# Two-layer graph and attention model on one core: last linear pair by pair, ScalarE's stores behind its copies, gate rows padded to 128

## What is computed

```python
# layer 0: capacity routing
probs = softmax(x @ router_gate);  topw, topi = top_k(probs, 2)
gates = zeros((T, E)).at[arange(T)[:, None], topi].set(topw / (topw.sum(-1, keepdims=True) + 1e-9))
top_g, tok_idx = top_k(gates.T, cap)          # the cap best tokens of each expert
...
# layer 1: the last linear of the graph network, then routing
out = h @ W_self1 + mean @ W_neigh1 + b1      # mean @ W_neigh1 is the last linear, "wn1"
x = x + out + attention(...)
scores = layernorm(x) @ gate_w.T;  top_k(scores, 2); softmax over the two
```

## Time and profile before

| | before |
|---|---|
| median of three runs | 3286.52 us (3283.59 to 3288.06) |
| the profiled execution, its time | 3286.96 us |
| its span, first to last instruction | 3285.1 us |
| mean granted TensorE clock | 0.949 of full |
| TensorE busy | 3052.6 us, 93% of the span |
| VectorE busy | 2019.8 us, 61% |
| ScalarE busy | 1263.2 us, 38% |
| GpSimd busy | 450.1 us, 14% |

### The profile page before, as it was taken

How to read it: one execution, slowest core, us unless ns; L and a number is a source line. 1 busy time by engine, 2 the same in 40 slices (tenths; PEclk the granted TensorE clock), 3 DMA queues, 4 the chain that set the end, 5 groups by cost and what they waited for, 6 DMA issues and landing times.

```text
span 3285.1 us, 53213 instructions
## 1 busy us (share of the span) xinstructions
PE 3052.6 (93%) x22308; PEld 2820.9 (86%) x22308; DVE 2019.8 (61%) x3533; ACT 1263.2 (38%) x2163; POOL 450.1 (14%) x327
## 2 busy tenths in 40 slices
PE   6999999999998899999599999999998999979997
PEld 6998897389987698988499998999998899978887
DVE  6986477977885645444466555766255653645665
ACT  4453055444421034433244334544134421424554
POOL 1033443443000111201000000000000000002222
PEclk9999999999998599999799999999999999968999
DMA  7322112132053266745621000462321333147997
GB/s 251 119 57 43 1 19 54 1 67 67 1 134 114 56 159 175 195 135 155 169 68 40 27 28 28 125 156 79 77 82 62 97 79 104 57 143 229 262 269 208
DMA packets 261920, 344.44 MB, mean 105 GB/s; under 512 B 40706, under 2 KB 223016, under 8 KB 259988
## 3 DMA queue, kind: packets, MB, share of 16 engines
q1 hardware_dynamic: 163351, 191.08, 19.4%
q0 software_dynamic: 43312, 77.14, 11.9%
q10 hardware_dynamic: 54989, 72.35, 7.3%
HBM read 264.10 MB, written 76.40 MB: 104 GB/s over the span
## 4 chain that ended last, share of the span: by engine, by line
PE 86%; DVE 7%; ACT 2%; issue 2%; DMA 1%; ACTq 1%; POOL 0%; DVEq 0%; SPq 0%; POOLq 0%
PE PV L475 18%; PE PV L476 17%; PE PV L477 17%; PE PV L579 6%; PE PS L475 3%; PE PS L476 3%; PE PS L477 3%; PE PV L849 3%; PE PA L503 1%; DVE b L1980 1%; PE PV L755 1%; PE PA L616 1%; DVE b_split L1682 1%; PE PV L795 1%; PE PA L770 1%
## 5 line engine op out<-in xcount | busy, mean ns | idle before, releaser
L475 PE MATMUL PV<-WH,b_split 128*125 128x256 f32 (+2 forms) x3708 | 1086.1, 293 | 94.2 <-DVE b_split L1682 73.9
L476 PE MATMUL PV<-WH,b_split 128*125 128x256 f32 (+2 forms) x3708 | 1073.5, 290 | 2.5 <-issue 2.5
L477 PE MATMUL PV<-WH,b_split 128*125 128x256 f32 (+2 forms) x3708 | 1072.2, 289 | 0.0
L1682 DVE TENSOR_TENSOR b_split<-b,b_split 128x500 fp32r<-128x500 f32 x1040 | 687.7, 677 | 424.5 <-ACT b_split L1288 411.3
L1288 ACT CAST b_split<-b 128x500 fp32r<-128x500 f32 x1040 | 626.0, 613 | 786.0 <-PE PV L477 732.2
L475 PEld LDWEIGHTS PV<-WH,b_split 128*125 128x125 f32 (+2 forms) x3708 | 698.3, 188 | 118.8 <-issue 72.3
L476 PEld LDWEIGHTS PV<-WH,b_split 128*125 128x125 f32 (+2 forms) x3708 | 701.6, 189 | 12.7 <-issue 2.7
L477 PEld LDWEIGHTS PV<-WH,b_split 128*125 128x125 f32 (+2 forms) x3708 | 698.6, 188 | 11.4
L1671 DVE TENSOR_TENSOR WH<-WS,WH 128x1024 fp32r<-128x1024 f32 x292 | 344.3, 1221 | 128.0 <-ACT WH L1278 126.7
L1278 ACT CAST WH<-WS 128x1024 fp32r<-128x1024 f32 x292 | 291.7, 1051 | 164.0 <-PE PV L579 143.2
L475 PE MATMUL PV<-b_split,WH 128*128 128x250 f32 (+3 forms) x1136 | 335.9, 296 | 7.6 <-DVE b_split L1682 6.4
(11 more groups left out here) (286 smaller groups left out, 3581.5 us busy)
## 6 DMA issues: line engine op xcount, KB each, us to landing
WS<-in_L_ffn_w SPq DMA_DIRECT2D x46, 1024.0 KB
WH<-at_d SPq DMA_DIRECT2D x15, 1093.8 KB
WS<-in_L_ffn_gate_w SPq DMA_DIRECT2D x16, 1024.0 KB
WS<-in_L_ffn_up_w SPq DMA_DIRECT2D x16, 1024.0 KB
WS<-in_L_ffn_down_w SPq DMA_DIRECT2D x16, 1024.0 KB
b<-key_d POOLq DMA_DIRECT2D x4, 2560.0 KB, 9.2
WS<-in_L_mix_Wv SPq DMA_DIRECT2D x8, 1024.0 KB
WS<-in_L_mix_Wk SPq DMA_DIRECT2D x8, 1024.0 KB
```

Of the source, the lines that this page charges most:

```text
L475: pe.matmul(o, a[0], b[0], start=start, stop=False, **kw)
L476: pe.matmul(o, a[0], b[1], start=False, stop=False, **kw)
L477: return pe.matmul(o, a[1], b[0], start=False, stop=stop, **kw)
L1682: ve.tensor_tensor(lo, src, hi.bitcast(F32), ALU.subtract).then_inc(xl_done, 1)
```

## The change

Three edits. First, in the last linear of layer 1 the third and the fourth column quarter are no longer done one after the other: from bank 10 on, each row pair gets its third and then its fourth quarter (`by_row`). The fourth quarter's weights are therefore split at piece 43 (`unit_due`). TensorE does the transposes of pair b - 1 behind the third-quarter bank of pair b and its router matmuls behind the fourth-quarter bank. Second, ScalarE's copies of transposed blocks come ahead of its stores: in layer 1 for every pair, at another place in the piece loop, in layer 0 for the last pair alone. Third, `gatesT` has 128 partitions in place of 8; GpSimd zeroes them all once (128x5000, `gz_ready`), VectorE waits for that before it writes rows 0 to 7, and the rank matmuls run over 128 rows of which 120 are zero.

```diff
@@ -212,10 +212,19 @@
         def unit_parts(u):
             return WH[:, u.place % 2, 0:UNIT], WH[:, u.place % 2, UNIT:2 * UNIT]
 
-        def row_pieces(at):
+        by_quarter = [(q, b) for q in range(NQ) for b in range(NB)]
+        by_row = by_quarter[0:(NQ - 2) * NB] + [(q, b) for b in range(NB) for q in (NQ - 2, NQ - 1)]
+
+        def row_pieces(at, order=by_quarter):
 
             return [cols(at)[:, 4 * kh:4 * kh + 4, i * R:(i + 1) * R]
-                    for q in range(NQ) for i in range(NT) for kh in range(2)]
+                    for _, b in order for i in (2 * b, 2 * b + 1) for kh in range(2)]
+
+        def unit_due(j, order):
+
+            if order is by_row and j >= (NQ - 2) * NPIECE:
+                return j == (NQ - 2) * NPIECE + 3
+            return j % NPIECE == 8
...
 
-        gatesT = FR[0:E, B2:B2 + 4 * T].rearrange("p (a t) -> p a t", t=T)
+        gates_all = FR[:, B2:B2 + 4 * T]
+        gatesT = gates_all.rearrange("p (a t) -> p a t", t=T)
...
@@ -505,33 +515,31 @@
                 if b == NB - 1:
                     mm.then_inc(rt_full, 1)
 
-            def linear_rows(name, bias=True, lead=None, between=None):
+            def linear_rows(name, bias=True, lead=None, between=None, order=by_quarter):
...
+                opened = {}
+                for m, (q, b) in enumerate(order):
+                    if lead is not None and q == 0:
+                        lead(b)
+                    if b == 0:
+                        opened[q] = unit("split")
+                    w = [h.rearrange("p (k n) -> p k n", k=KD) for h in unit_parts(opened[q])]
+                    bank = two(v.take(pe))
...
+                    if between:
+                        between(m)
+                    if b == NB - 1:
+                        opened[q].end = (v_full, v.n)
...
@@ -955,18 +963,15 @@
             either(lambda dt: neighbours_cols((rows(B2, FR), rows(B1, FR)), 4 * NT, dt))
             mark["agg2"] = v.n
 
-            def norm_1(n):
-
-                b = n - (NQ - 1) * NB
-                if b >= 2:
-                    turn_pair(1, b - 2)
-                if b >= 3:
-                    route_pair(1, b - 3)
-
-            linear_rows("wn1", bias=False, between=norm_1)
-            route_pair(1, NB - 3)
-            turn_pair(1, NB - 2)
-            route_pair(1, NB - 2)
+            def norm_1(m):
+
+                q, b = by_row[m]
+                if b and q == NQ - 2:
+                    turn_pair(1, b - 1)
+                if b and q == NQ - 1:
+                    route_pair(1, b - 1)
+
+            linear_rows("wn1", bias=False, between=norm_1, order=by_row)
             turn_pair(1, NB - 1)
             route_pair(1, NB - 1)
...
@@ -1189,6 +1194,7 @@
 
 
             pool.wait_ge(rt_full, 1)
+            pool.memset(gates_all.bitcast(F32), 0.0).then_inc(gz_ready, 1)
...
-            def hi_pieces(views, lead=None, extra=None, first=0):
+            def hi_pieces(views, lead=None, extra=None, first=0, order=by_quarter):
                 for j, src in list(enumerate(views))[first:]:
                     if lead and j < NPIECE and j % 4 == 0:
                         lead(j // 4)
-                    if j % NPIECE == 8:
+                    if unit_due(j, order):
                         next_unit()
                     hi_piece(src)
...
@@ -1553,8 +1559,10 @@
                 if c:
                     routed_pair(0, c - 1)
                 ln_sqrt(c)
-                store_normed(0, c)
+                if c < NB - 1:
+                    store_normed(0, c)
             routed_pair(0, NB - 1)
+            store_normed(0, NB - 1)
 
 
             pe_ = rbf[0:R, 512:512 + NT * E]
@@ -1630,19 +1638,21 @@
 
             def norm_1(j):
 
+                m = piece_at(j, 6)
+                q, b = by_row[m] if m is not None and m < NQ * NB else (0, 0)
+                if q == NQ - 2 and b:
+                    routed_pair(1, b - 1)
+                    store_normed(1, b - 1)
                 m = piece_at(j, 8)
-                b = -1 if m is None else m - (NQ - 1) * NB
-                if b >= 1:
-                    store_normed(1, b - 1)
-                    routed_pair(1, b - 1)
-                if b >= 0:
+                q, b = by_row[m] if m is not None else (0, 0)
+                if q == NQ - 1:
                     ln_sqrt(b)
 
-            linear_residual(B3, xs_d, also=norm_1, first=EARLY)
+            linear_residual(B3, xs_d, also=norm_1, first=EARLY, order=by_row)
             for j in (NQ * NPIECE, NQ * NPIECE + 4):
                 norm_1(j)
+            routed_pair(1, NB - 1)
             store_normed(1, NB - 1)
-            routed_pair(1, NB - 1)
...
             ve.tensor_tensor(gts[:, 0, :, :], gts[:, 0, :, :], pr, ALU.add).then_inc(gates_ready, 1)
+            ve.wait_ge(gz_ready, 1)
             for a in range(3):
                 for g in range(3):
                     w = min(4, NT - 4 * g) * R
                     at, bank = slice(4 * g * R, 4 * g * R + w), v.read(ve)[0:E, 0:w]
                     if a:
-                        emptied(ve.tensor_copy(gatesT[:, 1 + a, at], bank))
+                        emptied(ve.tensor_copy(gatesT[0:E, 1 + a, at], bank))
                         continue
-                    d(ve.tensor_copy(gatesT[:, 0, at], bank))
+                    d(ve.tensor_copy(gatesT[0:E, 0, at], bank))
                     d.sync()
-                    emptied(ve.tensor_tensor(gatesT[:, 1, at], bank, gatesT[:, 0, at].bitcast(F32), ALU.subtract))
+                    emptied(ve.tensor_tensor(gatesT[0:E, 1, at], bank, gatesT[0:E, 0, at].bitcast(F32),
+                                             ALU.subtract))
...
-            add_last = add_residual(B1, False)
+            add_last = add_residual(B1, False, order=by_row)
 
             def add_and_norm(m):
 
                 add_last(m)
-                if m >= (NQ - 1) * NB:
-                    ln_routed(1, m - (NQ - 1) * NB)
-
-            lo_pieces(row_pieces(B3), add_and_norm, first=EARLY)
+                q, b = by_row[m]
+                if q == NQ - 1:
+                    ln_routed(1, b)
+
+            lo_pieces(row_pieces(B3, by_row), add_and_norm, first=EARLY, order=by_row)
```

More of the change, by code:

```diff
@@ L400, in build @@
         qf_full, qf_done, tenths_ready = (sem(n) for n in ("qf_full", "qf_done", "tenths_ready"))
-        rank_full, rank_used = sem("rank_full"), sem("rank_used")
+        rank_full, rank_used, gz_ready = sem("rank_full"), sem("rank_used"), sem("gz_ready")
         kp_used, kv_free, qp_used, acc_free = (sem(n) for n in ("kp_used", "kv_free", "qp_used", "acc_free"))
@@ new lines, in linear_rows @@
+                opened = {}
[6 more added lines that the diff above has]
+                    bank = two(v.take(pe))
+                    for t in range(2):
+                        for kh in range(2):
+                            x = [h.rearrange("p (k t) -> p k t", k=4) for h in piece()]
+                            for k in range(4):
+                                mm = three(bank[0:R, t, :], [h[:, k, :] for h in x],
+                                           [h[:, 4 * kh + k, :] for h in w],
+                                           kh + k == 0, kh * 4 + k == KD - 1)
+                            piece_used(mm, t + kh == 2)
+                    if between:
+                        between(m)
+                    if b == NB - 1:
+                        opened[q].end = (v_full, v.n)
+                        if bias:
+                            bias_end.append(v.n)
@@ L1324, in piece_at, with residual_piece, linear_residual @@
                 return (j - lag) // 4 if j >= lag and (j - lag) % 4 == 0 else None
-            def residual_piece(src, m):
+            def residual_piece(src, m, order=by_quarter):
                 if m >= 4:
                     act.wait_ge(res_used, NQ * NB * n_res[0] + m - 3)
-                spread(act, two(RB[0:R, m % 4, :]), dpair(src, *divmod(m, NB)), res_full[m % 4])
-            def linear_residual(at, src, lead=None, store=None, also=None, first=0):
+                spread(act, two(RB[0:R, m % 4, :]), dpair(src, *order[m]), res_full[m % 4])
+            def linear_residual(at, src, lead=None, store=None, also=None, first=0, order=by_quarter):
                 def store_piece(m):
@@ L1340, in extra @@
                     if m is not None and m + 4 < NQ * NB:
-                        residual_piece(src, m + 4)
+                        residual_piece(src, m + 4, order)
                     m = piece_at(j, 10)
@@ L1350, in linear_residual @@
                 for m in range(4):
-                    residual_piece(src, m)
-                hi_pieces(row_pieces(at), lead=lead, extra=extra, first=first)
+                    residual_piece(src, m, order)
+                hi_pieces(row_pieces(at, order), lead=lead, extra=extra, first=first, order=order)
                 if store:
@@ L1682, in lo_piece, with lo_pieces @@
```

(6 more changed lines are left out.)

## The result

The changed kernel takes **3296.24 us** (median of 10 runs, 3288.68 to 3303.64), the kernel before 3287.2 us (10 runs). The ratio is 1.0022, 95% interval [1.0012, 1.0032]: 7 us slower by the ratio, 9 by the medians.

What follows compares the result with a forecast made beforehand. TensorE, busy 93% of the span, was taken to bound the kernel through waits, low clock and work others wait for. From 3286.96 us, +13 + 2 - 5.5 gave 3296.5, predicted as 3296 us, range 3279 to 3304.

Steps and rivals of the forecast that it cites:

- The wait in the last linear: Layer 1's last linear: eight ScalarE issues hold the cast, so TensorE stands 2.9 us four times, 11.6 us.
- the two small waits: Layer 1's last linear: 0.7 us for the first pair's norm and 0.5 us for the fourth quarter's weight split.
- The clock: Layer 1's last linear and routing: the clock falls behind waits; price 28.1 us, counted at 21.1, net +13 us.
- What falls in the wait stays low over the router group: Layer 1, each pair: low clock after the 2.9 us wait lasts, so a router group takes 6.89 instead of 3.40 us.
- Layer 0's stores: End of layer 0: issues behind the copies land the normed tiles later, delaying scores 1.1 to 3.3 us, taken as +2.
- The padding: Rank loop: 128 rows lift TensorE's clock and VectorE's waits go; gain 0 to 5.6 us, taken as -5.5.
- The prediction's sign for the loop: What would show it right in the rank loop: clock at 1.00 and a length of about 39 us.
- The rows count: Rank loop: clock 0.52 with 8 rows, 1.00 in a 64-row stretch, so 128 rows should lift it.
- The memset: Before the rank loop: zeroing gates takes 4.4 us, 3 covered by VectorE's small operations; it costs what sticks out.
- the holding clock: Rival, chance 0.20: the clock stays high in layer 1, which gains 7.9 us; 3275 us in all.
- the blocking memset: Rival, chance 0.10: VectorE's small operations wait for the memset, starting up to 4.4 us later; 3300 us.
- the padding doesn't lift the clock: Rival, chance 0.15: in the rank loop zeros do no work in the array; 3301.5 us.

Runs made afterwards that it cites:

- half: The changed kernel with four of each pair's eight layer 1 store issues left in place and four moved three pieces later; 3275.13 us, ratio 0.9956.
- late: The changed kernel with layer 1's stores of pairs 0 to 3 moved three pieces later; 3271.94 us, ratio 0.9954.
- layer1: The kernel before with only the new order of layer 1's last linear and its copies ahead of stores; 3299.88 us, ratio 1.0043.
- route: The changed kernel with each pair's router group moved behind the next pair's third-quarter bank, stores unmoved; 3288.65 us, ratio 1.0001.
- after: The changed kernel itself, all three edits against the kernel before; 3296.24 us, ratio 1.0022.
- l0: The kernel before with only layer 0's last four stores moved behind the copies; 3292.4 us, ratio 1.0009.
- pad32: The kernel before with only the gates padded, to 32 partitions; 3290.21 us, ratio 0.9997.
- pad64: The kernel before with only the gates padded, to 64 partitions; 3286.89 us, ratio 0.9998.
- warm: best2 with extra identity matmuls while TensorE waits for the last pair's norm (16) and ScalarE's first copies (5); 3272.79 us, ratio 0.9950.
- best2: late with layer 0's stores ahead of the copies again and the last pair's normed tiles stored before the accumulator starts; 3274.61 us, ratio 0.9948.

## Why the prediction was right

The forecast was 3296 us, slower by two opposite parts. Step by step:

**The wait in the last linear: right in kind and size.** Four waits of 2.9 us, 11.6 in all, were predicted; 11.5 were measured (2.6 to 3.1). half and late show that the issues cause them. Of the two small waits the one for the first pair's norm was put at 0.7 and measured 0.8; of the 0.5 for the weights the profile has nothing.

**The clock: right, and counted about right.** The price of falls everywhere was 28.1 us, of which I took 21.1. In the changed kernel's profile, each against its length at the high clock: router groups 6.7, 6.7 and 6.7 for 3.56 (9.5 us), single pieces (1.4), the dense banks 8.2, 7.6 and 8.5 for 5.9 (6.6), the last transposes and group 3.6 and 6.9 for 1.9 and 3.56 (5.0): 22.5. The last term was priced at 3.4, since 1.8 were to hide in the wait for the norm; nothing hid, since the transposes began behind that wait (1.98 us) and then took 3.59. A fall at the linear's very start, ahead of anything that the change moves, adds 1.5 (thirteen banks took 75.6 us, in late 74.1). Without both the stretch would be 180.5 - 22.5 - 1.5 = 156.5, 7.1 under before; predicted were 7.9. The sum for layer 1 was +13; the profile has +16.9 (15.4 without the fall at the start), layer1 +13.6. What a single run pays depends on where the falls land, as three slow groups here and two in layer1 show.

**"What falls in the wait stays low over the router group": shown, but not for every wait.** late (no wait, groups of 3.6 to 4.4) and route (waits, groups moved, 3.6 to 4.1) show it. Of the eight waits in after and layer1 five were followed by a slow group; what tells them from the other three stays open. Groups and transposes alone still bring two falls in late; the prediction names that source (layer 0, 1010 to 1013) but doesn't price it apart from the waits.

**Layer 0's stores: right, the mechanism too.** +2 (1.1 to 3.3) was predicted and the landing 6 to 8.2 us behind the fourth copy's start; l0 has 1046.93 to 1054.70, 7.8 us, and +2.7. In the profiled execution of the changed kernel a low clock hid it.

**The padding: right in kind, too small.** 5.5 us predicted, 7.6 measured in the loop. VectorE's waits for TensorE went as I summed (7.3 to 1.3, the page's groups), but its busy time fell too, from 38.68 to 37.01 us (38.64 and 38.68 in pad32 and pad64, where it waited as before). When it needn't wait, an instruction starts 0.08 us before the last one ends, and each of the nineteen waits that are gone had cost one such overlap, 1.5 us in all. The step that was short is the sum behind "at full clock VectorE sets the pace and the waits go": it left VectorE's own time as it was. (The prediction's sign for the loop, "about 39 us long", was nearer than its 5.5.)

```profile
L2239 DVE SCALAR_TENSOR_TENSOR b<-PV,wk,low 125x125 f32<-125x125 f32 x10 | 3.6, 355 | 1.3 <-PE PV L894 1.3
```

TensorE's step at full clock was put at 1.1 us, half of 2.2. It is 1.4 (27.88 / 20); VectorE's 1.85 (37.01 / 20) still sets the pace. The same shows in the first step of six matmuls, which ran at 1.00 in either kernel, with 8 rows before and with 128 now:

```profile
1066.33 1.42 PE L886 MATMUL PV<-b_split 8*125 8x512 f32 x6 [0.60 <-DVE RB L2210]
```

```profile
1073.65 1.41 PE L894 MATMUL PV<-b_split 128*125 128x512 f32 x6 [0.61 <-DVE RB L2222]
```

So 128 rows took no longer than 8, as the prediction had it.

**The reason given for the padding: in part a misreading.** "The rows count" was read from a stretch taken for 64-row matmuls, of which two thirds was 125-row work. By the same reasoning 64 rows would have been enough, and pad64 shows no gain. That rows count is right, and pad32 and pad64 show it; that the change had chosen 128 of them is what made this term come out, and that is luck.

**The memset was hidden.** 4.27 us against an estimate of 4.4, and from `scores` to the first write of gates there are 7.55 us in place of 7.45:

```profile
1058.88 4.27 POOL L1197 MEMSET b_split<- 128x5000 f32 x1 [249.27 <-PE PA L513]
...
1066.45 0.67 DVE L2216 CAST b_split<-PV 8x500 fp32r<-8x500 f32 x1 [1.16 <-PE PV L880]
```

Of the rivals, the holding clock and the blocking memset are refuted. That the padding doesn't lift the clock is refuted at 128 rows; at 32 and 64 rows it held.

**The sum.** 13 + 2 - 5.5 = 9.5 stood against 9.0 by the medians and 7.2 by the ratio. Layer 1 and the padding were each low in size in the profiles, with opposite signs, so that part of the agreement of the total is luck.

## What to carry to other kernels

An engine that issues DMAs is held up while it does: eight issues took 5.4 us here, in which nothing behind them in ScalarE's queue ran. Count how many pieces the consumer has in stock, and place such a block where what sticks out of that stock is nothing; moving half the block was already enough, and a block pushed too far back held the next copies. A reordering that puts thin matmuls and waits between dense ones should be priced at the low clock too: here the low clock cost 22.5 us in the changed kernel's profile and the waits 11.5. Where TensorE runs thin matmuls at the low clock and its result is waited for, try zero rows, all the way to 128: 64 gave nothing here. Read the shapes in a stretch before arguing from its clock.

## What the runs showed of the hardware

In one and the same loop the granted clock was 0.51 with 8 rows, 0.54 with 32, 0.55 with 64 and 1.00 with 128 rows, all but 8 of them zeros. TensorE was busy for 42 to 44 of 46 us in the first three, for 42.40 of 42.40 us at 0.50 with 8 rows, and for 27.88 of 38.35 in the last. So being busy was not what decided, and 120 rows of zeros were enough to hold the high clock. No run here has 128 rows of other data in this loop, nor a number between 64 and 128. The Trainium skill, TensorE: Matmul & The Clock Gate, section "Why this matters for your kernels", has full clock follow from being busy without gaps; these four runs disagree.

With identity matmuls in the wait, the last router group ran in 3.56 us (warm); without them it took 6.89 (best2), 4.8 (late) and 4.2 (half).

A memset of 4.27 us on GpSimd beside VectorE's small operations cost 0.1 us: from `scores` to the first write of gates there were 7.45 us before and 7.55 after.
